# Joined loop of a gated attention: the head variance spread by one block product, and its inverse root made on ScalarE

## The chip, the cores and the metric

The kernel runs on one core of a Trainium2 chip, as one launch. A core has five engines that each work through their own queue in order: TensorE (PE, matrix products into the eight banks of PSUM), VectorE (DVE), ScalarE (ACT), GpSimd (POOL) and SyncE (SP, which issues transfers here). They wait for each other at semaphores alone. The metric is the device time of one execution in microseconds (us); lower is better.

## The reference

Six blocks follow each other on 16 x 64 rows of 512 features. The change lies in the second, a gated linear attention of 16 heads; the third, a linear layer on quantised rows, is computed in the same loop. Cut to what matters:

```
# o: output of the scan, per head of 32 features, plus a sigmoid term
mu = o.mean(-1, keepdims=True)
var = o.var(-1, keepdims=True)
o = (o - mu) * lax.rsqrt(var + EPS)                 # EPS = 1e-5, over the 32 features of a head
o = o.transpose(0, 2, 1, 3).reshape(B, L, -1)
out = jax.nn.silu(g) * o @ Wout
x = x + out
# then, row by row
x = x + (mx_quantize(layernorm(x)) @ mx_quantize(weight).T + bias)   # blocks of 32, 6-bit grid
```

## The kernel before

The 1024 rows are cut into 8 groups of 128. The joined loop of `l0_gated_attention` takes them in a software pipeline: in pass t TensorE attends with group t-1 (`attend_pe`), makes the scores of group t (`scores_pe`), centres group t-1 (`mean_of_pe`), multiplies group t-3 with the output weights (`project_pe`), makes the variance of group t-1 (`variance_pe`), and from pass 5 on runs the linear layer for groups t-5 (`turn_blocks_pe`) and t-6 (`linear_pe`). The attended rows lie turned: the partitions are features, 32 for a head, and the free axis holds four tiles (C = 4) of 128 rows, 512 columns in all. Each engine's order is written out by hand in `tensor`, `vector`, `scalar` and `gpsimd`; `x.wait_ge(signal.s, signal(n))` waits until n+1 events of a signal have come.

How a group g gets its normalisation before the change:

1. `mean_of_pe` takes the head mean away (two products) into bank 5. ScalarE (`square_a`) copies the centred rows into `y` and squares them into `sq`; GpSimd (`gated_pool`) multiplies `y` with the gate.
2. `variance_pe`: four products with `sq` as the stationary side and four columns of `block` (1/32 in each 32 x 32 block of the diagonal) as the moving side. The result has rows on the partitions and 16 heads in 16 columns.
3. `variance_v` (VectorE, L1408) adds EPS into `var`, 128x16. `deviation_pool` (GpSimd, L1093) raises it to -0.5.
4. `widen_a` (ScalarE, L1666) repeats each of the 16 columns 32 times into `wide`, 128x512. `widen_pe` (TensorE, L1155) turns that with four transposes into bank 6.
5. `normal_v` (VectorE, L1413) multiplies `y` with bank 6. `project_pe` (L1163) multiplies the result with the output weights, in fp32, one product for each of the four tiles, into bank 7. `add_v` (L1417) adds that to the rows X, and `stats_of_v` starts the layer norm that feeds the quantisation.

Around this, VectorE masks the scores (`masked_v`), takes the low half of the attended rows (`low_of_v`, through the helper at L320), makes the last gate columns (`gate_last_v`, signal `sg_v`), splits the key weights of the next stage (`key_weights_v`, L320 with tile Wkv), quantises (`quantise_v`) and takes row statistics. ScalarE makes sigmoids of the value term (`sigmoid_a`, L1649), one group a pass, and the high half of the key weights (`key_weights_a`, helper L311). In pass 3 `widen_pe(0)` and `project_pe(0)` wait for the last gate columns. After pass 8 VectorE and TensorE run out the groups still in the pipeline (called the tail below), and the key products and row transposes of the next stage follow.

Other lines that rows name: L1127 and L1130 `attend_pe`, L1114 `scores_pe`, L1139 `mean_of_pe`, L1145 `variance_pe`, L1644 `gate_out_a`, L243 `normalise`, L281 the scaling in the quantisation, L227 row statistics, L1088 `gated_pool`, L1105 `bias_pool`. The tile names W and XT stand for several things: `y`, for one, is a part of W.

Of the kernel before, what the change touches and what calls it, by code (L numbers as in the profile page):

```python
# [13 lines left out]
P = 128  # L14
# [54 lines left out]
def build(nc, a, out):  # L69
# [12 lines left out]
    with ctx:  # L82
# [824 lines left out]
        def l0_gated_attention():  # L907
# [29 lines left out]
            var = sb(ph, "var", [P, 2, GH])  # L937
            half = sb(ph, "mhalf", [P, GH])
# [40 lines left out]
            wide_at = lambda g: y[:, 2, :] if g < 1 else wide[:]  # L979
# [24 lines left out]
            var_v = signal("b_var_v")  # L1004
            rst = signal("b_rst")
            wide_a = signal("b_wide_a")
            wide_pe = signal("b_wide_pe")
# [19 lines left out]
            def gpsimd():  # L1027
                for g in range(G):
                    row_stats_pool(1, g)
                p(pool.memset(half[:], -0.5))  # L1030
# [27 lines left out]
                for t in range(1, G + 1):  # L1058
# [5 lines left out]
                    deviation_pool(t - 1)  # L1064
# [25 lines left out]

            def deviation_pool(g):
                pool.wait_ge(var_v.s, var_v(g))
                pool.tensor_tensor(var[:, g % 2, :], var[:, g % 2, :], half[:], ALU.pow).then_inc(rst.s, 1)  # L1093
# [40 lines left out]
            def mean_of_pe(g):  # L1134
                pe.wait_ge(low_o.s, low_o(g))
                if g:
                    pe.wait_ge(var_v.s, var_v(g - 1))
# [20 lines left out]
            def project_pe(g):  # L1158
                pe.wait_ge(ynm.s, ynm(g))
                if g:  # L1160
                    pe.wait_ge(xsum.s, summed(2, g - 3) if g in (3, 4) else summed(1, g - 1))
                for c in range(C):
                    ins = pe.matmul(bank[:, 7, :], y[:, g % 3, c * P:(c + 1) * P], slot(7)[:, c, :], start=(c == 0), stop=(c == C - 1))  # L1163
                ins.then_inc(proj.s, 1)

            def turn_blocks_pe(g):

                pe.wait_ge(scaled.s, scaled(g))
                if g + 2 < G:
                    pe.wait_ge(ynm.s, ynm(g + 2))  # L1170
# [111 lines left out]
            def tensor():  # L1282
# [121 lines left out]
            def variance_v(g):  # L1404
                dve.wait_ge(var_pe.s, var_pe(g))
                if g >= 2:
                    dve.wait_ge(wide_a.s, wide_a(g - 2))
                dve.tensor_scalar(var[:, g % 2, :], bank[:, 5, 0:GH], EPS, None, ALU.add).then_inc(var_v.s, 1)  # L1408

            def normal_v(g):  # L1410
                dve.wait_ge(wide_pe.s, wide_pe(g))
# [1843 lines left out]
```

## Time and profile before

| | |
|---|---|
| runs | 1156.43, 1158.45, 1624.27 us; median 1158.45 |
| the profiled execution | 1155.84 us, its span 1154.6 us |
| TensorE clock granted | 0.999 of full speed |
| busy in the span | PE 1132.4 us (98%), DVE 749.6 (65%), ACT 537.2 (47%), POOL 244.3 (21%) |
| chain that ended last | PE 88%, DVE 6%, SP's queue 3% |
| the joined loop | first scores at 231.4 us, last key products ahead of the next stage's rows end near 346 us |

The profile is one execution. Busy time of an engine is the time in which an instruction of it ran; the chain is followed back from the last instruction, at each step to what released it. Times of rows are microseconds from the start of the span. TensorE's rows overlap, since products are pipelined: the start of one to the start of the next is what one costs, not its length. An fp32 product is two records and an fp32 transpose one.

### The profile page before, as it was taken

What the parts mean: (1) busy time and instruction counts of PE and PEld (TensorE: products, weight loads), DVE (VectorE), ACT (ScalarE), POOL (GpSimd) and SP (SyncE); (2) the same over time, 40 slices, a digit from 0 to 9 for tenths busy, and PEclk for the clock granted to TensorE, in tenths of its full rate; (3) what the DMA queues carried; (4) which work ended last, traced back from release to release, by engine and by line L of the source; (5) the groups of instructions that cost most, each with busy time, mean ns of one, the idle gap of its engine ahead of it and who ended that gap; (6) DMA issues with size and microseconds to landing.
All of it is one profiled execution on the core that took longest, in us unless ns stands there. A gap on an engine that the chain in (4) does not pass through costs nothing.

```text
span 1154.6 us, 21737 instructions
## 1 busy us (share of the span) xinstructions
PE 1132.4 (98%) x8721; PEld 845.5 (73%) x8721; DVE 749.6 (65%) x1524; ACT 537.2 (47%) x1037; POOL 244.3 (21%) x308
## 2 busy tenths in 40 slices
PE   7999999999999999999999999999999999999997
PEld 4665488776658777777777777777888778887886
DVE  6367478769894656666566666666797876546632
ACT  3244457653222655656565656565554532223421
POOL 2300013266740432121212122221432100000000
PEclk9999999999999999999999999999999999999999
DMA  9759710110205264444444444454810502224211
GB/s 351 273 212 404 278 55 1 40 44 1 110 19 183 40 137 100 92 92 93 92 93 93 92 92 99 91 101 79 112 19 1 83 5 33 37 37 76 34 37 37
DMA packets 325671, 111.57 MB, mean 97 GB/s; under 512 B 301834, under 2 KB 302908, under 8 KB 321348
## 3 DMA queue, kind: packets, MB, share of 16 engines
q1 hardware_dynamic: 324224, 109.11, 37.4%
q8 instruction: 69, 1.13, 0.4%
q10 hardware_dynamic: 1348, 1.09, 0.4%
q14 instruction: 30, 0.25, 0.1%
HBM read 65.59 MB, written 20.97 MB: 75 GB/s over the span
## 4 chain that ended last, share of the span: by engine, by line
PE 88%; DVE 6%; SPq 3%; DMA 1%; issue 1%; ACT 1%; POOL 0%; DVEq 0%; ACTq 0%
PE bank L303 64%; SPq L1871 3%; PE bank L1972 3%; PE bank L583 2%; PE bank L601 2%; PE bank L1988 2%; PE bank L1163 2%; PE bank L259 2%; PE bank L519 1%; PE bank L1185 1%; PE bank L1130 1%; PE bank L1127 1%; PE bank L1114 1%; PE bank L2445 1%; DVE xT L320 1%
## 5 line engine op out<-in xcount | busy, mean ns | idle before, releaser
L1909 POOL COPY PT<-W 32x512 f32<-32x512 f32 x120 | 83.8, 698 | 308.3 <-DVE W L2122 243.4
L2111 DVE CUSTOM_DVE_ANT_0 W<-bank,W 128x512 f32<-128x512 f32 x128 | 80.8, 687 | 101.8 <-PE bank L1972 98.2
L2202 ACT ACTIVATE K<-bank,vecT 128x512 f32<-128x512 f32 x64 | 43.8, 689 | 164.1 <-PE bank L303 164.1
L2223 ACT ACTIVATE W<-W,low 128x512 f32<-128x512 f32 x128 | 90.7, 711 | 16.9 <-DVE low L2111 16.9
L303 PE MATMUL bank<-xT,wT 128*128 128x512 f32 x384 | 92.6, 390 | 0.4 <-DVE wT L320 0.3
L303 PE MATMUL bank<-Wkv,Wq 128*128 128x512 f32 x384 | 92.7, 395 | 0.0
L303 PE MATMUL bank<-Wkv,ctxT 128*128 128x512 f32 x384 | 92.0, 394 | 0.0
L303 PE MATMUL bank<-ctxT,Wkv 128*128 128x512 f32 x384 | 90.1, 392 | 1.2 <-DVE ctxT L320 1.2
L303 PE MATMUL bank<-Wq,Wkv 128*128 128x512 f32 x384 | 89.8, 390 | 0.0
L303 PE MATMUL bank<-woT,hR 128*128 128x512 f32 x384 | 87.8, 390 | 0.6 <-DVE W_late L3081 0.5
L303 PEld LDWEIGHTS bank<-Wkv,ctxT 128*128 128x128 f32 x384 | 70.8, 188 | 22.2 <-ACT K L2202 5.7
L303 PEld LDWEIGHTS bank<-Wkv,Wq 128*128 128x128 f32 x384 | 70.6, 188 | 22.1 <-ACT K L2202 6.5
L303 PEld LDWEIGHTS bank<-ctxT,Wkv 128*128 128x128 f32 x384 | 71.4, 188 | 17.5 <-issue 3.0
L2229 ACT ACTIVATE W<-W,total 128x512 f32<-128x512 f32 x128 | 82.0, 712 | 4.8 <-DVE total L2117 4.8
L303 PEld LDWEIGHTS bank<-woT,hR 128*128 128x128 f32 x384 | 71.9, 188 | 16.4 <-DVE W_late L3081 0.9
L303 PEld LDWEIGHTS bank<-xT,wT 128*128 128x128 f32 x384 | 71.8, 188 | 16.6 <-issue 1.1
L303 PEld LDWEIGHTS bank<-Wq,Wkv 128*128 128x128 f32 x384 | 71.8, 188 | 15.6 <-issue 0.8
L235 POOL TENSOR_TENSOR rstd<-rstd,half_pow 128x1 f32<-128x1 f32 x48 | 30.4, 634 | 212.8 <-DVE rstd L231 212.8
L2122 DVE STREAM_TRANSPOSE W<-W 128x512 f32<-128x512 f32 x120 | 74.5, 675 | 0.2 <-ACT W L2229 0.2
L3185 ACT ACTIVATE h<-bank,vecT 128x512 f32<-128x512 f32 x32 | 22.1, 689 | 89.2 <-PE bank L303 59.9
L303 PE MATMUL bank<-z,BT 128*128 128x512 f32 x192 | 49.1, 391 | 0.6 <-ACT h L3185 0.4
L303 PEld LDWEIGHTS bank<-z,BT 128*128 128x128 f32 x192 | 35.8, 188 | 9.1 <-ACT h L3185 1.8
(378 smaller groups left out, 2117.6 us busy)
## 6 DMA issues: line engine op xcount, KB each, us to landing
PT<-W SPq DMA_DIRECT2D x360, 64.0 KB, 2.1
W<-ctx_turned SPq DMA_DIRECT2D x16, 1024.0 KB, 5.9
W<-in_ctx_dram SPq DMA_DIRECT2D x8, 1024.0 KB, 10.6
ctx_turned<-ctxT SPq DMA_DIRECT2D x8, 1024.0 KB, 7.6
ctx_turned<-W SPq DMA_DIRECT2D x8, 1024.0 KB, 6.7
XT<-in_ctx_dram SPq DMA_DIRECT2D x4, 1024.0 KB, 11.6
XT<-in_L_ffn_wi_dram SPq DMA_DIRECT2D x64, 64.0 KB, 2.1
raw_own<-in_ctx_dram SPq DMA_DIRECT2D x3, 1024.0 KB, 11.0
```

Of the source, the lines that this page charges most:

```text
L235: ins = pool.tensor_tensor(rstd[:, g:g + 1], rstd[:, g:g + 1], half_pow[:], ALU.pow)
L259: ins = pe.transpose(bank[:, first + r, to:to + 32], src_of(t, k)[strip, :], ident[strip, strip])
L303: ins = pe.matmul(dst, stationary(x, k), moving(y, k), start=(first and n == 0), stop=(last and n == len(passes) - 1), skip_group_check=True)
L583: ins = pe.matmul(bank[b * NP:(b + 1) * NP, 4, :], q2T[:, c, j * P + b * NP:j * P + (b + 1) * NP], ctxT[j % 2][:, b, c, :], start=(c == 0) ...
L1871: sp.dma_start(there, here).then_inc(pt_in[half].s, 16)
L1909: pool.tensor_copy(there, here).then_inc(kept_p.s, 1)
L1972: ins = pe.matmul(bank[s2 * NP:(s2 + 1) * NP, 4 + r, :], qT[strip, 2 * rnd + s2, i * NP:(i + 1) * NP], K[strip, 2 * rnd + s2, :], start=Tr ...
L2111: dve.tensor_tensor_reduce(out=PR[:, j, :], in0=bank[:, 4 + j % 4, :], in1=mask, scale=1.0, scalar=3.0e38, op0=ALU.add, op1=ALU.min, accum ...
L2122: dve.transpose(PR[:, j, :], PR[:, j, :]).then_inc(probs.s, 1)
L2202: act.activation(K[:, m, :], bank[:, n % 4, :], ACT.Identity, bias=pcol("L1_xattn_bk", m)).then_inc(ring_a.s, 1)
L2223: act.activation(PR[:, j, :], PR[:, j, :], ACT.Exp, bias=low[:, j:j + 1], scale=-1.0, accum_out=total[:, j:j + 1]).then_inc(expd.s, 1)
L2229: act.mul(PR[:, t, :], PR[:, t, :], total[:, t:t + 1]).then_inc(scaled_p.s, 1)
```

## The change

- `variance_pe` is one product: `block` as the stationary side, `sq` as the moving side, 128x512 in fp32. It gives the variance of each head already repeated on the 32 features, turned as `y` is.
- ScalarE makes the inverse root, with EPS as the bias, into `wide` (now called root). For groups 0 and 1 it copies the variance first (`variance_a`, L1639 of the changed kernel) and takes the root in `early_root_a` (L1646); for the others it takes it straight from bank 5 (L1642), after `normal_v` of the group before has read the buffer.
- `widen_pe`, `widen_a`, `variance_v` and `deviation_pool` are gone.
- `normal_v` reads the root from SBUF. It is made a pass earlier: in pass t for group t-2, and for group 0 at the end of pass 2.
- `project_pe` of groups 0 to 2 is split: its first chunk stands ahead of the mean.
- The sigmoids are all made by pass 2, and the key weights of the next stage a pass later (chunk 0 at the end of pass 2).

```diff
             def variance_pe(g):
                 pe.wait_ge(sqr.s, sqr(g))
-                for t in range(C):
-                    ins = pe.matmul(bank[:, 5, 4 * t:4 * t + 4], sq_at(g)[:, t * P:(t + 1) * P], block[:, 0:P:GDV], start=True, stop=True)
-                ins.then_inc(var_pe.s, 1)
-
-            def widen_pe(g):
-                pe.wait_ge(wide_a.s, wide_a(g))
-                if g:
-                    pe.wait_ge(ynm.s, ynm(g - 1))
-                if g >= 3:
-                    pe.wait_ge(xt_a.s, xt_a(G + g - 3))
-                for t in range(C):
-                    ins = pe.transpose(bank[:, 6, t * P:(t + 1) * P], wide_at(g)[:, t * P:(t + 1) * P], ident[:])
-                ins.then_inc(wide_pe.s, 1)
+                pe.matmul(bank[:, 5, :], block[:], sq_at(g), start=True, stop=True).then_inc(var_pe.s, 1)
...
                 for t in range(G + 3):
                     if t == 1:
                         gate_pe(5)
-                    if t == 3:
-                        pe.wait_ge(sg_v.s, sg_v(1))
-                        widen_pe(0)
                     if 1 <= t <= G:
                         attend_pe(t - 1)
-                    if 4 <= t < G + 3:
-                        widen_pe(t - 3)
...
+                    if t == 3:
+                        pe.wait_ge(sg_v.s, sg_v(2))
+                    if 3 <= t < 6:
+                        project_pe(t - 3, range(1))
                     if 1 <= t < 6:
                         mean_of_pe(t - 1)
...
-                    if t == 3:
-                        pe.wait_ge(sg_v.s, sg_v(2))
                     if 3 <= t:
-                        project_pe(t - 3)
+                        project_pe(t - 3, range(1, C) if t < 6 else range(C))
...
             def normal_v(g):
-                dve.wait_ge(wide_pe.s, wide_pe(g))
+                if g < 2:
+                    dve.wait_ge(root_a.s, root_a(g))
+                else:
+                    dve.wait_ge(var_a.s, var_a(g))
                 dve.wait_ge(gated.s, gated(g))
-                dve.tensor_tensor(y[:, g % 3, :], y[:, g % 3, :], bank[:, 6, :], ALU.mult).then_inc(ynm.s, 1)
+                dve.tensor_tensor(y[:, g % 3, :], y[:, g % 3, :], root_at(g), ALU.mult).then_inc(ynm.s, 1)
...
+            def variance_a(g):
+                act.wait_ge(var_pe.s, var_pe(g))
+                if g < 2:
+                    act.copy(root_at(g), bank[:, 5, :]).then_inc(var_a.s, 1)
+                else:
+                    act.wait_ge(ynm.s, ynm(g - 1))
+                    act.activation(root_at(g), bank[:, 5, :], ACT.Abs_reciprocal_sqrt, bias=eps[:]).then_inc(var_a.s, 1)
+
+            def early_root_a(g):
+                act.wait_ge(var_a.s, var_a(g))
+                act.activation(root_at(g), root_at(g), ACT.Abs_reciprocal_sqrt, bias=eps[:]).then_inc(root_a.s, 1)
...
-                    if t + 1 < G:
-                        sigmoid_a(t + 1)
-                    if 2 <= t < G + 2:
-                        widen_a(t - 2)
+                    if t == 1:
+                        sigmoid_a(2)
+                    elif t == 2:
+                        sigmoid_a(6)
+                        sigmoid_a(7)
                     if t <= G:
                         square_a(t - 1)
                     if t <= 2:
                         gate_out_a(5 + t)
+                    if t == 1:
+                        for g in (3, 4, 5):
+                            sigmoid_a(g)
+                    elif t == 2:
+                        early_root_a(0)
                     if t >= 5:
                         blocks_a(t - 5)
-                    if t <= C:
-                        key_weights_a(t - 1)
+                    if 3 <= t <= 5:
+                        key_weights_a(t - 2)
+                    if t <= G:
+                        variance_a(t - 1)
+                    if t == 2:
+                        early_root_a(1)
+                        key_weights_a(0)
```

The order on TensorE from the variance of group 1 (end of pass 2) to that of group 2 (end of pass 3), before; L1155 is the widening, L1163 the projection:

```order
L1145 MATMUL bank<-block,W 128x4 [waits b_sqr]
L1145 MATMUL bank<-block,W 128x4 x3
L1155 MATMUL bank<-ident,W 128x128 [waits b_wide_a,b_sg_v]
L1155 MATMUL bank<-ident,W 128x128 x3
L1127 MATMUL bank<-Am,V 32x128 [waits c_o_v,b_sig,b_asb]
L1127 MATMUL bank<-Am,V 32x128 x15
L1130 MATMUL bank<-ident,XT 128x128 x4
L1114 MATMUL bank<-W 128x256 [waits b_asb]
L1114 MATMUL bank<-W 128x256 x7
L1139 MATMUL bank<-oT,centring 128x512 [waits b_var_v,c_o_v]
L1139 MATMUL bank<-oT,centring 128x512
L1163 MATMUL bank<-W_early,W 128x512 [waits b_y,b_sg_v]
```

The same place in the changed kernel; L1136 is the variance, L1144 the projection and L1131 the mean:

```order
L1136 MATMUL bank<-W,block 128x512 [waits b_sqr]
L1119 MATMUL bank<-Am,V 32x128 [waits c_o_v,b_sig,b_asb]
L1119 MATMUL bank<-Am,V 32x128 x15
L1122 MATMUL bank<-ident,XT 128x128 x4
L1106 MATMUL bank<-W 128x256 [waits b_asb]
L1106 MATMUL bank<-W 128x256 x7
L1144 MATMUL bank<-W_early,W 128x512 [waits b_y,b_sg_v]
L1131 MATMUL bank<-oT,centring 128x512 [waits b_var_a,c_o_v]
L1131 MATMUL bank<-oT,centring 128x512
L1144 MATMUL bank<-W_early,W 128x512 x3
L1136 MATMUL bank<-sq,block 128x512 [waits b_sqr]
```

The widening ahead of the attention is gone, and a chunk of the projection, which waits for `b_y` (the signal of `normal_v`), has moved ahead of the mean. The order on ScalarE from the gate of pass 2 to the attended rows of group 2 (oT), before:

```order
L1644 ACTIVATE sgT<-bank,vecT 128x512 [waits proj]
L311 CAST Wkv<-W 128x512 [waits slot_in_5]
L311 CAST Wkv<-W 128x512 [waits slot_in_6]
L1653 CAST oT<-bank 128x512 [waits b_ot_pe]
L1649 ACTIVATE XT<-XT 128x512 [waits b_wv]
```

And in the changed kernel, where L1618 is the gate:

```order
L1618 ACTIVATE sgT<-bank,vecT 128x512 [waits proj]
L1646 ACT_TABLE_LOAD
L1646 ACTIVATE W<-W,eps 128x512 [waits b_var_a]
L1639 COPY wide<-bank 128x512 [waits b_var_pe]
L1646 ACTIVATE wide<-wide,eps 128x512 [waits b_var_a]
L311 CAST Wkv<-W 128x512 [waits slot_in_5]
L311 CAST Wkv<-W 128x512 [waits slot_in_6]
L1627 CAST oT<-bank 128x512 [waits b_ot_pe]
```

A table load, two roots and a copy now stand between the gate and the casts of the key weights. It is the one table load that the changed kernel has more. The order on VectorE at the end of the loop, from the last row of the quantisation of group 4 (L285) to the first statistics of the tail, before:

```order
L285 TENSOR_SCALAR W<-XT 128x512 [waits d_scaled,dve_seq]
L1408 TENSOR_SCALAR var<-bank 128x16 [waits b_wide_a,b_var_pe]
L1417 TENSOR_TENSOR X<-X,bank 128x512 [waits proj]
L1413 TENSOR_TENSOR W<-W,bank 128x512 [waits b_gated,b_wide_pe]
L227 BN_STATS stats<-X 128x6 [waits xsum]
```

And in the changed kernel, with L1392 for `add_v` and L1388 for `normal_v`:

```order
L285 TENSOR_SCALAR W<-XT 128x512 [waits d_scaled,dve_seq]
L1392 TENSOR_TENSOR X<-X,bank 128x512 [waits proj]
L1388 TENSOR_TENSOR W<-W,wide 128x512 [waits b_gated,b_var_a]
L227 BN_STATS stats<-X 128x6 [waits xsum]
```

The row that waited for the variance is gone; `normal_v` is that of group 7 instead of 6, and waits for the root of the same group.

## Rows read from the trace of the kernel before

**Rows 1.** Windows: stretch, its length, busy us of each engine, clock, DMA.
```profile
core 0: us, PE busy (x) PEld busy (x) DVE busy (x) ACT busy (x) POOL busy (x), PEclk, DMA share, GB/s
254.00:313.00 59.00, 58.88 (x433) 36.81 (x433) 52.56 (x102) 18.46 (x34) 37.19 (x28) 1.00 0.15 55
313.00:340.00 27.00, 26.56 (x81) 12.70 (x81) 25.19 (x53) 7.11 (x13) 14.25 (x13) 1.00 0.07 20
```

**Rows 2.** Timeline of TensorE, pass 3: start, us, line, operation [idle before <-releaser].
```profile
249.17 0.95 PE L1145 MATMUL bank<-block,W 128*128 128x4 f32 x8
249.98 0.64 PE L1155 MATMUL bank<-ident,W 128*128 128x128 f32 x4
250.55 1.08 PE L1127 MATMUL bank<-Am,V 128*32 128x128 f32 x32
...
254.12 0.74 PE L1139 MATMUL bank<-oT,centring 128*128 128x512 f32 x2 [0.32 <-DVE oT L320]
254.80 3.67 PE L1163 MATMUL bank<-W_early,W 128*128 128x512 f32 x8
258.31 0.95 PE L1145 MATMUL bank<-block,sq 128*128 128x4 f32 x8
259.19 1.08 PE L1127 MATMUL bank<-Am,V 128*32 128x128 f32 x32
```

**Rows 3.** Timeline of ScalarE: a table load, and the gate of pass 2.
```profile
231.39 0.69 ACT L1644 ACTIVATE sgT<-bank,vecT 128x512 f32<-128x512 f32 x1 [2.52 <-PE bank L303]
232.10 1.28 ACT L1649 ACT_TABLE_LOAD   x1
233.39 0.63 ACT L1649 ACTIVATE XT<-XT 128x512 f32<-128x512 f32 x1
...
249.37 0.69 ACT L1644 ACTIVATE sgT<-bank,vecT 128x512 f32<-128x512 f32 x1 [0.98 <-PE bank L303]
249.96 1.13 ACT L311 CAST Wkv<-W 128x512 fp32r<-128x512 f32 x2
```

**Rows 4.** Timeline of VectorE, passes 2 and 3.
```profile
249.37 1.29 DVE L320 TENSOR_TENSOR Wkv<-W,Wkv 128x512 fp32r<-128x512 f32 x2 [0.80 <-PE bank L303]
250.58 0.74 DVE L1401 SCALAR_TENSOR_TENSOR sgT<-bank,vecT,sgT 128x512 f32<-128x512 f32 x1
...
253.98 0.68 DVE L1413 TENSOR_TENSOR W<-W,bank 128x512 f32<-128x512 f32 x1
```

**Rows 5.** Chain of waits, pass 4: start, us, what.
```profile
261.36 0.44 PE bank L1155 x4
```

**Rows 6.** Timelines of TensorE, VectorE and GpSimd, end of pass 8 and tail.
```profile
312.18 0.95 PE L1145 MATMUL bank<-block,sq 128*128 128x4 f32 x8
...
309.44 1.54 DVE L281 TENSOR_TENSOR XT<-XT,inv 128x512 f32<-128x512 f32 x1
...
313.17 0.17 DVE L1408 TENSOR_SCALAR var<-bank 128x16 f32<-128x16 f32 x1 [1.72 <-PE bank L1145]
313.26 0.68 DVE L1417 TENSOR_TENSOR X<-X,bank 128x512 f32<-128x512 f32 x1
...
314.45 0.69 DVE L227 BATCH_NORM_STATS2 stats<-X 128x6 f32<-128x512 f32 x1
...
317.20 1.16 DVE L243 TENSOR_SCALAR W<-X,mv,rstd 128x512 f32<-128x512 f32 x1
...
324.63 0.55 DVE L243 TENSOR_SCALAR XT<-X,mv,rstd 128x512 f32<-128x512 f32 x1 [0.59 <-POOL rstd L235]
...
309.17 1.27 POOL L1088 TENSOR_TENSOR W<-W,sgT 128x512 f32<-128x512 f32 x1 [0.94 <-ACT W L1659]
...
313.42 2.91 POOL L1093 TENSOR_TENSOR var<-var,mhalf 128x16 f32<-128x16 f32 x1 [0.85 <-DVE var L1408]
...
316.81 1.27 POOL L1105 TENSOR_TENSOR X<-X,W 128x512 f32<-128x512 f32 x1
```

More of the change, by code:

```diff
@@ L936, in l0_gated_attention @@
             w = sb(ph, "w2", [P, G, GH])
-            var = sb(ph, "var", [P, 2, GH])
-            half = sb(ph, "mhalf", [P, GH])
+            eps = sb(ph, "eps", [P, 1])
             def xb(h, c, lo, n):
@@ L978, in l0_gated_attention @@
             sq_at = lambda g: W[:, 0, 3, :] if g < 2 else sq[:]
-            wide_at = lambda g: y[:, 2, :] if g < 1 else wide[:]
+            root_at = lambda g: y[:, 2, :] if g < 1 else wide[:]
             by_group = lambda ap: ap.rearrange("f (c g r) -> f (c g) r", c=2, g=G)
@@ L1003, in l0_gated_attention @@
             var_pe = signal("b_var_pe")
[L1004 to L1007, printed above, removed]
+            var_a = signal("b_var_a")
+            root_a = signal("b_root_a")
             gated = signal("b_gated")
@@ L1029, in gpsimd @@
                     row_stats_pool(1, g)
-                p(pool.memset(half[:], -0.5))
+                p(pool.memset(eps[:], EPS))
                 p(pool.memset(augw[:], 0.0))
@@ L1089, in gated_pool @@
                                    ALU.mult).then_inc(gated.s, 1)
-            def deviation_pool(g):
-                pool.wait_ge(var_v.s, var_v(g))
-                pool.tensor_tensor(var[:, g % 2, :], var[:, g % 2, :], half[:], ALU.pow).then_inc(rst.s, 1)
             def scale_pool(g):
@@ L1136, in mean_of_pe @@
                 if g:
-                    pe.wait_ge(var_v.s, var_v(g - 1))
+                    pe.wait_ge(var_a.s, var_a(g - 1))
                 for h in range(2):
@@ L1143, in variance_pe, with project_pe @@
                 pe.wait_ge(sqr.s, sqr(g))
-                for t in range(C):
-                    ins = pe.matmul(bank[:, 5, 4 * t:4 * t + 4], sq_at(g)[:, t * P:(t + 1) * P], block[:, 0:P:GDV], start=True, stop=True)
-                ins.then_inc(var_pe.s, 1)
-            def widen_pe(g):
-                pe.wait_ge(wide_a.s, wide_a(g))
-                if g:
-                    pe.wait_ge(ynm.s, ynm(g - 1))
-                if g >= 3:
-                    pe.wait_ge(xt_a.s, xt_a(G + g - 3))
-                for t in range(C):
-                    ins = pe.transpose(bank[:, 6, t * P:(t + 1) * P], wide_at(g)[:, t * P:(t + 1) * P], ident[:])
-                ins.then_inc(wide_pe.s, 1)
[L1158 to L1164, printed above, removed]
+                pe.matmul(bank[:, 5, :], block[:], sq_at(g), start=True, stop=True).then_inc(var_pe.s, 1)
+            def project_pe(g, chunks=range(C)):
+                if 0 in chunks:
+                    pe.wait_ge(ynm.s, ynm(g))
+                    if g:
+                        pe.wait_ge(xsum.s, summed(2, g - 3) if g in (3, 4) else summed(1, g - 1))
+                for c in chunks:
+                    ins = pe.matmul(bank[:, 7, :], y[:, g % 3, c * P:(c + 1) * P], slot(7)[:, c, :], start=(c == 0),
+                                    stop=(c == C - 1), skip_group_check=True)
+                if C - 1 in chunks:
+                    ins.then_inc(proj.s, 1)
             def turn_blocks_pe(g):
                 pe.wait_ge(scaled.s, scaled(g))
-                if g + 2 < G:
-                    pe.wait_ge(ynm.s, ynm(g + 2))
                 if g:
@@ L1532, in vector @@
                         low_of_v(t - 1)
-                    if 3 <= t:
-                        normal_v(t - 3)
                     for r in range(4):
                         masked_v(t, r)
+                    if 3 <= t:
+                        normal_v(t - 2)
                     if t in (6, 7):
@@ L1545, in vector @@
                         gate_last_v(5 + t)
+                    if t == 2:
+                        normal_v(0)
                     if t in (3, 6, 7):
                         key_weights_v({3: 1, 6: 2, 7: 3}[t])
-                    if 1 <= t:
-                        variance_v(t - 1)
                     if 3 <= t:
@@ L1557, in vector @@
                 low_of_v(7)
-                normal_v(5)
+                normal_v(6)
                 quantise_v(4)
-                variance_v(7)
                 for g in (5, 6, 7):
                     add_v(g)
-                    if g < 7:
-                        normal_v(g + 1)
+                    if g == 5:
+                        normal_v(7)
                     stats_of_v(1, g)
@@ L1660, in square_a @@
                 act.activation(sq_at(g), bank[:, 5, :], ACT.Square).then_inc(sqr.s, 1)
-            def widen_a(g):
-                act.wait_ge(rst.s, rst(g))
-                if g:
-                    act.wait_ge(wide_pe.s, wide_pe(g - 1))
-                act.copy(wide_at(g).rearrange("p (h d) -> p h d", h=GH),
-                         var[:, g % 2, :].unsqueeze(2).broadcast_to([P, GH, GDV])).then_inc(wide_a.s, 1)
+            def variance_a(g):
[8 more added lines that the diff above has]
+                act.activation(root_at(g), root_at(g), ACT.Abs_reciprocal_sqrt, bias=eps[:]).then_inc(root_a.s, 1)
             def blocks_a(g):
@@ L1764, in scalar @@
                         gate_out_a(5 + t)
+                    if t == 1:
[3 more added lines that the diff above has]
+                        early_root_a(0)
                     if t >= 5:
                         blocks_a(t - 5)
-                    if t <= C:
-                        key_weights_a(t - 1)
+                    if 3 <= t <= 5:
+                        key_weights_a(t - 2)
+                    if t <= G:
+                        variance_a(t - 1)
+                    if t == 2:
+                        early_root_a(1)
+                        key_weights_a(0)
                     if t == G + 3:
```

6 lines of the change are left out of this document (removed).

## The prediction

> **What bounds the kernel now.** I read the page first: TensorE is busy 98% of the span and the chain that ended last is TensorE for 88%. The change touches one stretch of some 110 us of the 1154.6, so I asked for busy times by stretch. From 254 to 313 us, the middle of the joined loop, TensorE is busy 58.88 of 59 us and VectorE 52.56: TensorE sets the pace and VectorE is close behind. From 313 to 340 us both are nearly full, 26.56 and 25.19 of 27 [rows 1]. Who leads there is told by the chain of waits and the timeline of VectorE: VectorE waited 1.72 us for the narrow products of the last group, and from there the chain runs through VectorE and GpSimd [rows 6]. So two things count: TensorE's own time up to the last variance product, and how soon after it VectorE gets going.
>
> **TensorE's work.** A widening is four 128x128 transposes and is worth 0.44 us in the chain [rows 5]; its start-to-start time in the third pass is 0.57 us (249.98 to 250.55) [rows 2]. All eight go. Six of them (groups 0 to 5) stand ahead of the last variance product, two behind it. The four narrow variance products (128x4 out of 128x128 weights) take 0.88 us from start to start (258.31 to 259.19). The one product of 512 columns that replaces them is of the same kind as those of L1163, of which four take 3.51 us (254.80 to 258.31), so 0.88 us each [rows 2]. I cost this exchange at nothing; if the switch from one kind to the other costs or saves 0.1 us, eight make plus or minus 0.8 us.
>
> **The new wait in pass 3.** Before, TensorE waited 0.32 us here, for the low half of the attended rows (254.12) [rows 2]. Now the first chunk of the projection of group 0 stands ahead of the mean, and it waits for VectorE's `normal_v(0)`. That is queued behind `key_weights_v(0)` and `gate_last_v(7)`, and the key weights are now queued on ScalarE behind both early roots. Step by step:
> - ScalarE starts the gate of u=7 at 249.37 and takes 0.69 us. A table load followed such a gate 0.71 us after its start (231.39 to 232.10), and the next instruction started 1.29 us after the load (233.39) [rows 3]. So the load stands at 250.08 and the first root at 251.37.
> - A root reads a 128x512 tile with a bias from memory, as the gate does: 0.69 us, with the next start 0.6 us on (249.37 to 249.96) [rows 3]. No row shows this function; the bounds are the 0.63 us of the sigmoid, and 0.69. The copy of the variance of group 1 starts at 251.97 and ends at 252.60, since I give it the sigmoid's 0.63; the second root needs it and ends at 253.29.
> - The two casts of the key weights take 1.13 us together [rows 3], the first ending about 253.8, the second about 254.3.
> - VectorE's second split then ends about 255.0 (two take 1.29 us), the gate's product (0.74 us) about 255.65, and `normal_v(0)` (0.68 us) about 256.3 [rows 4].
>
> TensorE would be ready early: variance product of group 1 at 249.17, 0.88 us, then the 3.25 us that lie between 250.55 and 253.80 (254.12 less the wait), so 253.30 [rows 2]. It stalls 3.05 us, against 0.32 before. Then one chunk (0.88), the mean (0.68), three chunks (2.63): the variance product of group 2 starts at 256.35 + 4.19 = 260.5 instead of 258.31, so 2.2 us late [rows 2]. The low half of group 2 is late too, but VectorE makes it right after `normal_v(0)`, within the 0.88 us of the chunk.
>
> **Passes 4 to 8.** Five widenings go, 5 x 0.44 = 2.2 us. The normalisation of a group is now made a whole pass ahead of its projection, so no new stall. VectorE's work per pass is the same but for 0.17 us of the row that added epsilon (L1408, hidden today by other waits) [rows 6]. At the last variance product (312.18 before) the sum is 2.2 - 2.2 = 0, within 0.1.
>
> **The tail.** VectorE no longer waits for the variance before adding group 5, but `normal_v(7)`, the next row, does: product 312.18 + 0.88, some 0.15 to its end (the four narrow ones: start 312.18, used at 313.17), the root 0.69, so 313.9; the normalisation 0.6; statistics at 314.5, where they stand now (314.45) [rows 6]. So 0 again. What is left is GpSimd: without the power of 2.91 us at 313.42, the bias of group 4 (now 316.81) comes up to 0.8 us sooner, when the statistics it is queued behind are ready. Today it lies on the normalisation at 317.20, which takes 1.16 us where the one at 324.63 takes 0.55 [rows 6]. That frees between 0 and 0.6 us; I take 0.4, being nearer to the freed case. `normal_v(7)` also leaves its old place, 0.6 us later in the tail, but VectorE then waits for GpSimd (0.59 us at 324.63 [rows 6]), whose chain starts from the same quantisation, so I count nothing for it. Behind the loop there is no edit: the later stages start sooner by what the loop ends sooner, as TensorE has no idle time of size there.
>
> **The sum**: + 2.2 (pass 3) - 2.2 (widenings) + 0 (products) - 0.4 (collision gone) = -0.4 us, on the profiled execution's own 1155.84 (span 1154.6 and 1.2 around it): 1155.4. The three runs shown have the median 1158.45; the one of 1624.27 left out, the other two and the profiled one lie at 1155.84, 1156.43 and 1158.45, middle 1156.4. A median of undisturbed runs of the changed kernel should then be 1156.0.
>
> **What the skill says against it.** The table load took 1.28 us and the next instruction followed 0.01 us later; ahead of it stood 0.02 us [rows 3]. The Trainium skill (ScalarE: Activation LUTs, What ACT_TABLE_LOAD costs) gives 1283 ns for the load, which the row bears out, and 1380 ns of drain on top, which the row does not show. By its sum the stall of pass 3 would be 1.4 us longer and the total +1.0 us, an estimate.
>
> **Rivals.**
> - The stall is hidden (chance 0.15). If ScalarE's roots and casts came early enough, only the savings remain: 6 x 0.44 ahead of the last product plus the 0.32 us wait and 0.4, so -3.4 us: 1153.0 on the same footing. Against it: the chain has nine links in series and the first cannot start before 249.37.
> - Slower by a collision of memory reads (chance 0.13). `normal_v` read one operand from PSUM and took 0.68 us; now both lie in SBUF. The product of L281, which has both in SBUF, took 1.54 us at 309.44 beside GpSimd's gate at 309.17 [rows 6]. If `normal_v` met GpSimd's work at each of the last six groups, VectorE would need 6 x 0.86 = 5.2 us more, less the slack that it has in passes 4 to 8, 59 - 52.56 = 6.4 in all but mostly spent on waits in the first of them [rows 1]; about half would reach the end: +2.2 us, 1158.6. It decides from three hits in passes 6 to 8. Against it: GpSimd has been relieved of 2.91 us a pass. In a sentence of its own: the Trainium skill (GPSIMD Engine Reference, Specifications) names just this sharing for VectorE instructions with two SBUF inputs; the row at 309.44 agrees.
> - The load costs as a drained switch does (chance 0.1). If the first root starts 1.4 us later than the row of 232.10 says, each link behind it does too: +1.0 us, 1157.4.
> - The change has no further effect than to trade waits, and the collision of 317.20 stays (chance 0.12): 0 to +0.3 us, 1156.5.
>
> That leaves 0.5 for the forecast.
>
> **How the numbers follow.** The bounds of the unknown costs are 0.8 us either way for the products and 0.4 for the roots; the likeliest case spans 1154.5 to 1157.5. With the hidden stall below and the collision above, and the 2.6 us over which the undisturbed runs of before spread, the range is 1152.5 to 1160. Within 2% means 23 us, about what a measurement of this kernel can tell from no change; no case reaches a sixth of it. The loop would have to lose or gain a fifth of its length, which only a mechanism that I don't see could do: same 0.98, faster 0.01, slower 0.01.
>
> **What would show it.** In the profile after: no L1155-like transposes in the loop beyond the turned blocks; one more table load on ScalarE near 250.1 with no gap behind it; TensorE idle about 3 us near 253.3, ended by VectorE's normalisation; the variance product of group 2 near 260.5, and that of group 7 near 312.2; the second statistics of the tail near 314.5; a wait on the root ahead of the normalisation of group 7; the normalisation near 317 at about 0.55 us. The forecast is wrong if that stall is under 2 us or over 4, if the wide product takes other than 0.8 to 1.0 us, or if `normal_v` takes over 1 us in passes 6 to 8.

## The result and the profile after

The changed kernel takes 1160.76 us (median of 7 runs, 1159.22 to 1161.61) against 1156.86 for the kernel before (median of 7, of which one took 1624.27), a ratio of 1.0034 with the interval 1.0023 to 1.0045. It is slower by 3.9 us, within 2%, where I forecast 0.4 us less and a range that ended at 1160. The profiled execution has a span of 1159.5 us against 1154.6.

The time that TensorE waited, summed by what it waited for, the three longest waits of the changed kernel:

```profile
engine line waited for: us in total, times, longest us
PE bank L513 <- DMA W<-in_L_xattn_kernel_k_dram: 9.4, 1, 9.4
PE bank L1144 <- DVE W L1388: 3.3, 1, 3.3
PE bank L1978 <- issue: 2.3, 3, 0.9
```

The same view of the kernel before:

```profile
PE bank L513 <- DMA W<-in_L_xattn_kernel_k_dram: 7.7, 1, 7.7
...
PE bank L1988 <- issue: 1.1, 2, 0.8
```

The first row, the load at the very start, is chance: in the run `after_again` below the same kernel had its first product at 7.75 us, like the kernel before at 7.68. The rows of the loop stand 2.6 us late in the profiled execution after: 1.7 us from this load, and 0.9 us that came between the first product and the first attend product (228.54 us apart, 227.63 before and 227.68 in `after_again`). So I compare from the first attend product on (237.94 us; 235.32 before). The second row is the stall that I forecast. The third I had not thought of: TensorE stands in the attention of a later stage (L1978, L1988 before) and waits for nothing that the profile shows.

The stall in pass 3, timeline of TensorE after (start, us, line, operation [idle before <-releaser]):

```profile
254.91 1.15 PE L1106 MATMUL bank<-W 32*128 32x256 f32 x16
259.31 1.10 PE L1144 MATMUL bank<-W_early,W 128*128 128x512 f32 x2 [3.26 <-DVE W L1388]
259.85 1.02 PE L1131 MATMUL bank<-oT,centring 128*128 128x512 f32 x2
260.70 2.73 PE L1144 MATMUL bank<-W_early,W 128*128 128x512 f32 x6
263.28 1.02 PE L1136 MATMUL bank<-sq,block 128*128 128x512 f32 x2
```

Timelines of ScalarE and VectorE after, the chain that makes it:

```profile
252.76 1.28 ACT L1646 ACT_TABLE_LOAD   x1
254.06 0.72 ACT L1646 ACTIVATE W<-W,eps 128x512 f32<-128x512 f32 x1
254.69 0.57 ACT L1639 COPY wide<-bank 128x512 f32<-128x512 f32 x1
255.28 0.72 ACT L1646 ACTIVATE wide<-wide,eps 128x512 f32<-128x512 f32 x1
255.91 1.12 ACT L311 CAST Wkv<-W 128x512 fp32r<-128x512 f32 x2
...
256.61 1.29 DVE L320 TENSOR_TENSOR Wkv<-W,Wkv 128x512 fp32r<-128x512 f32 x2 [5.35 <-ACT Wkv L311]
257.82 0.74 DVE L1379 SCALAR_TENSOR_TENSOR sgT<-bank,vecT,sgT 128x512 f32<-128x512 f32 x1
258.49 0.68 DVE L1388 TENSOR_TENSOR W<-W 128x512 f32<-128x512 f32 x1
```

VectorE is idle for 5.35 us behind a table load, a copy, two roots and a cast, and TensorE for 3.26 us behind VectorE. Against [rows 2] the variance product of group 2 starts 2.35 us later (counted from the first attend product, as all shifts here). It is 1.91 us late in pass 4, 1.83 in pass 5, then 1.46, 1.10 and 0.73 at group 7. The tail, timeline of VectorE after, for the last rows of [rows 6]:

```profile
317.31 0.69 DVE L1388 TENSOR_TENSOR W<-W,wide 128x512 f32<-128x512 f32 x1 [0.89 <-ACT wide L1642]
317.92 0.69 DVE L227 BATCH_NORM_STATS2 stats<-X 128x6 f32<-128x512 f32 x1
...
320.68 0.54 DVE L243 TENSOR_SCALAR W<-X,mv,rstd 128x512 f32<-128x512 f32 x1
```

Here the statistics are 0.86 us late, the normalisation takes 0.54 us where it took 1.16, and the next stage's first query product is 0.23 us late. So in this execution the loop costs 0.23 us. But the kernel is 3.9 us slower: most of the loss is elsewhere.

### The profile page after: what moved, and what is told of

The parts are those of the page before. It is cut to its first block, busy times and chain, and to the rows that moved or that the text cites. A ratio compares the mean times of both kernels' runs of the same rounds, so it can differ in the third digit from the quotient of the medians.

```text
span 1159.5 us, 21548 instructions
## 1 busy us (share of the span) xinstructions
PE 1130.4 (97%) x8641; PEld 838.1 (72%) x8641; DVE 749.1 (65%) x1516; ACT 539.9 (47%) x1040; POOL 222.9 (19%) x300
## 3 DMA queue, kind: packets, MB, share of 16 engines
q8 instruction: 69, 1.13, 0.4%
## 4 chain that ended last, share of the span: by engine, by line
PE 89%; DVE 6%; SPq 2%; ACT 1%; DMA 1%; issue 1%; POOL 0%; DVEq 0%; ACTq 0%
PE bank L303 65%; PE bank L1962 3%; PE bank L583 2%; PE bank L601 2%; PE bank L1978 2%; PE bank L259 2%; SPq L1861 2%; PE bank L1144 1%; PE bank L519 1%; PE bank L1166 1%; DMA W<-in_L_xattn_kernel_k_dram 1%; DVE stats L227 1%; PE bank L249 1%; PE bank L2435 1%; PE bank L1122 1%
```

## The experiments

The ratios are to the kernel before, measured in the same session and on the same chip (1156.65 to 1156.69 us in the three sessions). "Loop" is the time from the first attend product to the first query product of the next stage; "behind the loop" is from there to the start of TensorE's last product.

### Both kernels again

No edit.

> The kernel before, unchanged, profiled once more: how much of the 4.9 us between the two profiled executions is one execution against another. Theory O (the opening is chance): the first weight load (6.3 us to landing before, 8.0 after) and with it TensorE's first row (7.7 us before, 9.4 after) vary from execution to execution, here anywhere from 7.5 to 9.5. Rival (the opening goes with the program): again within 0.3 us of 7.7. Theory F (instruction fetch): TensorE's idle times in the attention of the next stage, behind no wait, come back at the same places as before (435.5, 522.1, 549.3 us, 1.6 us in all), since the instruction stream is the same. Ratio 1.000 +- 0.001.

> The changed kernel, unchanged, profiled once more. Theory O: TensorE's first row anywhere from 7.5 to 9.5 us. Rival: again near 9.4. Theory F: TensorE's idle times behind no wait come back at the same places (418.2, 746.9, 774.2, 803.9 us, 2.8 us in all), apart from a common shift. Ratio to before about 1.003.

Before again: 1156.66 us. After again: 1160.14 us, 1.0031 (1.0019 to 1.0043). Loop 120.46 us before (120.44 in the first profile), 122.34 after, where the first profile of the same kernel had 120.67. Timeline of TensorE, `after_again`:

```profile
256.81 1.21 PE L1144 MATMUL bank<-W_early,W 128*128 128x512 f32 x2 [3.26 <-DVE W L1388]
257.34 1.53 PE L1131 MATMUL bank<-oT,centring 128*128 128x512 f32 x2
258.67 3.94 PE L1144 MATMUL bank<-W_early,W 128*128 128x512 f32 x6
```

The stall is 3.26 us as before, but the same six product records take 3.94 us and not 2.73. Windows over these products (stretch, its length, busy us by engine, PEclk, DMA), of `after_again`:

```profile
256.80:262.40 5.60, 5.59 (x10) 2.71 (x11) 5.32 (x8) 2.11 (x4) 1.81 (x1) 0.70 0.01 3
...
258.00:260.00 2.00, 2.00 (x5) 1.15 (x4) 2.00 (x4) 1.09 (x3) 0.43 (x1) 0.50 0.00 0
```

and of the first profile of the changed kernel:

```profile
259.30:263.30 4.00, 3.99 (x11) 2.00 (x12) 4.00 (x6) 2.11 (x4) 1.28 (x1) 1.00 0.00 0
```

The granted clock fell to half (0.50 is the level of 1.2 GHz) behind the stall in one execution and not in the other, and it costs 1.67 us (122.34 - 120.67). The Trainium skill (TensorE: Matmul & The Clock Gate, Part 1) says of the slow products at a kernel's start that their number differs from run to run of the same kernel; these two profiles show the like behind a stall in the middle of one.

The first product came at 7.68 and 7.75 us in these two. In the other runs it came between 7.45 and 7.83 us, but at 9.45 in `after_filled`: the late opening is chance and goes with neither kernel.

### The position of TensorE's instruction stream

The two rows of "issue" above stand at different times in the two kernels. The page lists a DMA queue that brings instructions, the same row in both kernels:

```profile
q8 instruction: 69, 1.13, 0.4%
```

69 pieces in 1.13 MB are 16 KB each. The trace of the changed kernel has 17606 instructions of TensorE, which makes 64 bytes an instruction and 256 instructions a piece. The change takes 169 instructions out of TensorE's stream (80 products with their weight loads, and 9 waits), so every piece boundary behind the loop moves. In `after_pad169` they are given back as waits that are met long before, spread over the wide products of the loop (two calls of `wait_ge` become one instruction, hence the factor 2 in the code; the trace has 492 waits for 323); `before_pad87` puts 87 into the kernel before, which is the same position as taking 169 away, as a piece holds 256 (256 - 169 = 87).

```diff
+            padded = {"left": 169, "sites": 64}
+            def pad_pe():
+                n = -(-padded["left"] // padded["sites"]) if padded["sites"] else 0
+                padded["left"] -= n
+                padded["sites"] -= 1
+                for _ in range(2 * n):
+                    pe.wait_ge(ready_v.s, ready_v(2))
...
+                    pad_pe()
                     ins = pe.matmul(bank[:, 7, :], y[:, g % 3, c * P:(c + 1) * P], slot(7)[:, c, :], start=(c == 0),
```

> The changed kernel with 169 waits that are long met, spread ahead of the 64 wide products of the joined loop, so that TensorE's stream has as many instructions ahead of the next stage as before the change (it has 169 fewer: 80 weight loads, 80 products, 9 waits). Nothing computed is changed. Theory F: the idle times of 0.7 to 0.9 us at 746.9, 774.2 and 803.9 go and those of the kernel before come in their place (near 435, 522 and 549): 1.0 to 2 us faster than the changed kernel, ratio to before 1.0015 to 1.0025. Rival (the waits or transfers of the next stage are late for another reason than the fetch): same idle times as after, ratio 1.0034 or more, as the waits cost up to 0.05 us each where nothing hides them.

> The kernel before with 87 such waits in the joined loop. A fetch brings 256 instructions, and 169 fewer stand at the same place in a fetch as 87 more. Theory F: the next stage then shows the idle times of the changed kernel (three of 0.7 to 0.9 us near 745, 771 and 800) and loses those near 435, 522 and 549: 1 to 2 us slower than before, ratio 1.001 to 1.002. Rival: idle times as before, ratio 1.000.

After with 169: 1158.30 us, 1.0015 (1.0006 to 1.0025), so 1.8 us less than the changed kernel. Before with 87: 1159.20 us, 1.0025 (1.0016 to 1.0034), so 2.5 us more than the kernel before (forecast 1 to 2), with no useful work changed; its loop keeps 120.32 us. Timeline of TensorE in the changed kernel, the attend product of the later stage near 745 us:

```profile
744.07 1.99 PE L1978 MATMUL bank<-PT,V 128*32 128x64 f32 x126
746.92 0.27 PE L1978 MATMUL bank<-PT,V 128*32 128x64 f32 x2 [0.87 <-issue]
```

The same place in `after_pad169`:

```profile
745.27 1.99 PE L1990 MATMUL bank<-PT,V 128*32 128x64 f32 x128
747.19 0.50 PE L303 MATMUL bank<-Wkv,Wq 128*128 128x512 f32 x1
```

And `before_pad87`, which has the kernel before's code but stands at the changed kernel's places, and at one more near 438 us:

```profile
438.40 0.54 PE L2000 MATMUL bank<-PT,W 128*32 128x64 f32 x22 [1.16 <-issue]
...
745.26 0.27 PE L2000 MATMUL bank<-PT,V 128*32 128x64 f32 x2 [0.90 <-issue]
...
772.51 0.31 PE L2000 MATMUL bank<-PT,W 128*32 128x64 f32 x5 [0.73 <-issue]
```

In such a block 128 products of 64 columns and their weight loads, 256 instructions, run in 2 us. The idle time comes 2 products ahead of the block's end or 5, to the same number in `before_pad87` and in the changed kernel.

That TensorE waits there for the next piece of its program is borne out by a count over all fourteen profiles of this document. They have 38 idle times of over 0.25 us without a wait behind the loop. Count TensorE's instructions (products, weight loads, waits) that were recorded ahead of each: 8642 and 9154 in the kernel before, 12737, 13249 and 13762 in the changed one, 10177, 10690 and 11202 in `keys_spread_p113` below. Divided by 256, all 38 counts leave 193 or 194. And all 38 idle times end 2.2 to 2.9 us after the transfer of a piece has begun (after: begun at 744.25, end of the idle time at 746.92). What no run shows is why only a few of the 69 pieces come late, and how late: at one place (8642) three executions of one stream stood for 0.34, 0.72 and 0.32 us (before, before again, and `before_late0` below), and at the place of 438 us the changed kernel did not stand, where `late_keys` and `keys_spread` below, with as many instructions ahead, stood for 1.16.

So the number of instructions ahead decides where TensorE can stand, and this is worth up to 2.5 us here. The time behind the loop is 791.8 and 792.4 us (before, before again), 793.2 and 793.5 (after, again), 792.1 (after with 169), 794.2 (before with 87); the idle times over 0.25 us make up most of these differences, not all. (`before_late0`, with the stream of before, has 790.7.)

### The clock behind the stall

`after_filled` lets TensorE work while it would stand, and releases nothing sooner. The three products go to a free bank and are not read.

```diff
                     if t == 3:
+                        pe.wait_ge(sg_v.s, sg_v(1))
+                        for _ in range(3):
+                            pe.matmul(bank[:, 6, :], ident[:], slot(7)[:, 0, :], start=True, stop=True,
+                                      skip_group_check=True)
                         pe.wait_ge(sg_v.s, sg_v(2))
```

> The changed kernel with three wide fp32 products of no use (the identity with a chunk of the out weights, into a bank that is free then), put on TensorE ahead of the wait of the first out product, so that TensorE works through about 2.7 of the 3.26 us in which it stood; nothing is released sooner. Theory (the slow products behind the stall come from the granted clock, which falls after TensorE has stood for 3.26 us): the clock is 1.00 from 255 to 264 us, the six out products take 2.7 us and not 3.94, the loop takes 120.7 us and not 122.3, and the time is 1158.5 us against 1160.2. Rival 1 (they were slow for another reason, such as reads of the same memory by the engines that run then): they stay at 3.9 us, time 1160.2. Rival 2 (the fillers end later than the wait): slower than 1160.2 by what they overrun.

1157.62 us, 1.0010 (1.0001 to 1.0019): 2.5 us less than the changed kernel, for more work. Timeline of TensorE, and in a second fence the window behind the wait:

```profile
255.36 2.84 PE L1306 MATMUL bank<-W_early,ident 128*128 128x512 f32 x6
258.69 1.10 PE L1144 MATMUL bank<-W_early,W 128*128 128x512 f32 x2 [0.49 <-DVE W L1393]
```

```profile
258.70:262.70 4.00, 4.00 (x11) 2.00 (x12) 4.00 (x7) 2.11 (x4) 1.27 (x1) 1.00 0.00 0
```

Full clock, loop 120.66 us. The forecast of 1158.5 was 0.9 high; the filling also moves the stream, by 12 instructions in the trace, and of the three idle times of the later stage the one near 803 us (0.72) is gone.

`before_late0` puts a stall into the kernel before:

```diff
                     if 3 <= t:
+                        if t == 3:
+                            for _ in range(5):
+                                v(dve.tensor_tensor(xq[:, 0, :], X[:, 0, :], X[:, 0, :], ALU.add))
                         normal_v(t - 3)
```

> The kernel before with five additions of no use (X+X into free rows, 128x512, 0.69 us each) on VectorE ahead of the first normalisation (normal_v(0) in pass 3), so that the ready normalised group, and TensorE's first out product, come about 3.4 us late; nothing else is changed, and the instruction stream of TensorE is the one before. Theory (the stall by itself costs its own length and, in most executions, the clock behind it): TensorE idle 3.2 to 3.6 us ahead of the first out product, granted clock near 0.5 for 3 to 5 us behind it, loop 120.4 + 3.4 + 1.7 = 125.5 us, time 1161.8 us. Rival (a stall of this length is made up by TensorE's slack in passes 4 to 8, or the clock fell for another reason that only the changed kernel has): clock 1.00 throughout, loop 120.4 to 123.8 us, time 1157 to 1160.

1163.57 us where 1161.8 was forecast, 1.0062 (1.0049 to 1.0075), loop 127.09. The five additions took 4.53 us, not 3.4. Timeline of TensorE, and in a second fence the window over the products:

```profile
259.15 5.70 PE L1163 MATMUL bank<-W_early,W 128*128 128x512 f32 x8 [4.53 <-DVE W L1413]
```

```profile
259.10:264.70 5.60, 5.55 (x9) 2.41 (x10) 3.50 (x6) 0.00 (x0) 0.00 (x0) 0.63 0.01 3
```

The eight records took 3.67 us in [rows 2] and take 5.70 here. Loop: 120.44 + 4.53 + 2.03 = 127.00. Nothing of the stall was made up in passes 4 to 8, and nothing of the changed kernel is needed for the clock to fall.

### The stall itself

`late_keys` takes the cause of the stall out of pass 2.

```diff
                     if t == 2:
                         dve.wait_ge(proj.s, proj(GATE + 7))
-                        key_weights_v(0)
...
-                    if t in (3, 6, 7):
-                        key_weights_v({3: 1, 6: 2, 7: 3}[t])
+                    if t in (3, 4, 6, 7):
+                        key_weights_v({3: 0, 4: 1, 6: 2, 7: 3}[t])
...
-                    if 3 <= t <= 5:
-                        key_weights_a(t - 2)
+                    if 3 <= t <= 6:
+                        key_weights_a(t - 3)
...
                         early_root_a(0)
-                        key_weights_a(0)
```

> The changed kernel with the four chunks of key weights rounded and split one pass later (chunk 0 in pass 3 and not in pass 2), so that in pass 2 ScalarE goes from the two early roots straight to the attended copy and VectorE does not wait for the rounded key weights ahead of its gate and its first normalisation; all else as in the changed kernel. Theory (the stall and what hangs on it is one of two causes): TensorE's idle time ahead of the first out product falls from 3.26 us to under 0.8, no stretch behind it is granted less than the full clock, and the loop (first attend product to the first query product) takes near 119 us in place of 122.3 (120.7 in the execution without the clock loss); the time is 1155.5 us (1160.2 - 3.0 - 1.7), and the products of the later stages where TensorE stands without a wait (746, 773, 803 us) still do so, 3 us earlier. Rival (VectorE bounds the loop in passes 4 to 8, busy 9.7 us in ten): the stall goes, but the loop's end comes no more than 1 us earlier, and the time is 1158.5 or more.

> The kernel of the run late_keys with 169 long-met waits spread ahead of 64 wide products of TensorE's loop, as in after_pad169, which bring the instruction stream behind the loop back to the positions it has in the kernel before. Theory (the two causes, the stall in the loop and the position of the stream, are separate and add up): 1.8 us below late_keys (after_pad169 against after_again: 1158.3 against 1160.1), 1153.7 us, faster than both kernels; idle without a wait at 521 and 549 us, none at 743 to 801. Rival (the two share a cause, or the waits cost time of their own in a loop that has no stall): the same as late_keys or slower.

1158.19 us (1.0012, 1.0004 to 1.0021) and 1156.52 us (1.0000, 0.9991 to 1.0009). Both forecasts failed, by 2.7 and 2.8 us (1155.5 and 1153.7). The stall in pass 3 is gone, but the loop takes 119.85 us, not 119.0, and with 169 waits 121.48; behind the loop `late_keys` takes 794.2 us, with the 1.16 us near 438.7 told of above. Timelines of TensorE and VectorE in `late_keys`, two passes later (VectorE's split stands at the end of pass 4):

```profile
272.17 1.10 PE L1144 MATMUL bank<-W_early,W 128*128 128x512 f32 x2 [1.58 <-DVE X L1392]
273.84 0.73 PE L1131 MATMUL bank<-oT,centring 128*128 128x512 f32 x2 [0.57 <-DVE oT L320]
...
269.29 2.14 DVE L320 TENSOR_TENSOR Wkv<-W,Wkv 128x512 fp32r<-128x512 f32 x2
271.35 0.68 DVE L1392 TENSOR_TENSOR X<-X,bank 128x512 f32<-128x512 f32 x1
```

I had put a split into pass 4, where VectorE has none in either kernel: it took 2.14 us (1.29 in pass 2; GpSimd was at work all through it, from 269.45 to 272.55), `add_v(1)` behind it was late, and the next out product needs its bank. A wait was traded for another. In the run with 169 waits the clock fell behind these waits (there 1.53 and 0.61 us) too:

```profile
272.00:279.00 7.00, 6.39 (x15) 3.04 (x14) 6.79 (x14) 2.60 (x5) 1.95 (x3) 0.76 0.01 2
```

`keys_spread` moves the splits on, with the cast order of `late_keys`; the other two differ from it in the position of the stream alone.

```diff
-                    if t in (3, 4, 6, 7):
-                        key_weights_v({3: 0, 4: 1, 6: 2, 7: 3}[t])
+                    if t in (3, 6, 7):
+                        key_weights_v({3: 0, 6: 1, 7: 2}[t])
...
                 normal_v(6)
                 quantise_v(4)
+                key_weights_v(3)
```

> As late_keys, but VectorE splits the key weights' chunks 0 to 3 in passes 3, 6, 7 and behind pass 8 (between the last normalisation of a group's rows there and add_v(5)), not in passes 3, 4, 6 and 7. Theory (late_keys lost its gain to VectorE: the split put into pass 4 took 2.14 us, so that add_v(1) was late, and with it TensorE's out product of group 2 by 1.58 us and the mean of group 4 by 0.57): both idle times go, the loop takes near 117.8 us in place of 119.85, and the time is 1156.0 us against late_keys' 1158.2. Rival (VectorE bounds these passes as a whole, and the wait comes back in a later pass or in the tail): loop 119.5 or more and time 1158.

> keys_spread with 169 long-met waits in TensorE's loop, so that the instruction stream behind the loop stands where it does in the kernel before. Theory: 1.8 to 2 us below keys_spread by the position of the stream, near 1154.1 us, which is 0.998 of the kernel before. Rival (the waits cost time where TensorE does not stand): the same as keys_spread.

> keys_spread with 113 such waits in place of 169: only the position of the stream differs. Theory (TensorE's idle times without a wait follow from where the pieces of 256 instructions fall in the dense attend products): the loop is that of keys_spread_p169 within 0.1 us, the idle times without a wait are at other places or of other lengths than with 0 and with 169 waits, and any difference of the times is their sum. No size is forecast from outside: the three positions measured so far differ by 0 to 2.5 us, so 1153.5 to 1157. Rival (the waits' number costs, not the position): between keys_spread and keys_spread_p169.

1156.05 us (0.9993, 0.9984 to 1.0002), 1153.29 us (0.9975, 0.9965 to 0.9985) and 1156.10 us (0.9998, 0.9989 to 1.0006). The loops are 117.79, 117.78 and 117.73 us, so all the rest lies behind them: 794.2, 792.0 and 794.7 us. The forecasts were 1156.0, 1154.1 and 1153.5 to 1157. It is the position and not the number of the waits that counts, for 113 of them gave nothing and 169 gave 2.8 us. With 113 waits the three idle times lie in stretches where none lay before. Timeline of TensorE, `keys_spread_p113`:

```profile
602.57 0.31 PE L1989 MATMUL bank<-PT,W 128*32 128x64 f32 x6 [1.28 <-issue]
...
632.78 0.53 PE L1989 MATMUL bank<-PT,V 128*32 128x64 f32 x21 [1.16 <-issue]
...
660.28 0.54 PE L1989 MATMUL bank<-PT,W 128*32 128x64 f32 x24 [1.09 <-issue]
```

and `keys_spread_p169`, at the places of the kernel before:

```profile
519.65 0.42 PE L1989 MATMUL bank<-PT,V 128*32 128x64 f32 x12 [0.70 <-issue]
...
546.89 0.43 PE L1989 MATMUL bank<-PT,W 128*32 128x64 f32 x15 [0.79 <-issue]
```

`keys_spread_p169` is 3.4 us faster than the kernel before and 7 us faster than the changed one.

### The sum closed

`after_filled` with 156 waits: the stall stays, the clock is held, the stream stands as before.

> The changed kernel with the three useless products in the stall (as after_filled) and 156 long-met waits, which with the 13 instructions that the filling adds bring the stream's position behind the loop to that of the kernel before; the stall itself stays. Theory (the whole loss of the change is the clock behind the stall and the position of the stream; the stall's length and the saved widenings cancel, as forecast): within 1 us of the kernel before, 1156.7 to 1157.2 us, loop 120.7, clock 1.00 from 250 to 270 us, idle without a wait near 523 and 551 us only. Rival (something else in the changed kernel costs as well): 1158 or more.

1156.83 us, 0.9999 (0.9990 to 1.0008), loop 120.55. Idle without a wait at the places of the kernel before alone. (The filling and the waits make 168 instructions in the trace, one short of 169.) With the clock and the stream put right the changed kernel is the kernel before, to 0.2 us. By medians the stream is worth 1.8 us (1160.14 to 1158.30) and the clock, at this position of the stream, 1.5 (1158.30 to 1156.83).

## Why the prediction was wrong, step by step

- **Behind the loop: this step failed.** "The later stages start sooner by what the loop ends sooner" is not so. I read it from the absence of large idle times and looked for edits only. The 169 instructions that the change takes out of TensorE's program shift where it stands in the dense attend blocks: 1.8 us (1160.14 against 1158.30).
- **The stall's price: half of this step failed.** The stall came with the links in the order that I gave: forecast 3.05 us, measured 3.26; group 2's variance product forecast 2.2 us late, measured 2.35. I charged it its length. It also costs TensorE's clock: 1.7 us where it fell (122.34 against 120.67), 1.5 in the medians. With the 1.8 above that is 3.3 to 3.5 us, of the 1160.14 - 1156.65 = 3.5 measured.
- **Passes 4 to 8: right in kind, too large.** Forecast -2.2 us, measured 2.35 - 0.73 = 1.62. Pass 4 gave the 0.44. Pass 5 gave 0.08, for the mean of its pass waited for VectorE's low half: from the first chunk of the projection to the variance product TensorE took 4.83 us (275.54 to 280.37), 0.28 more than for the same products before (271.38 to 275.93). "No new stall" was wrong there. The last three gave 0.36 or 0.37 each.
- **The exchange of products, costed at nothing**, is at most 0.1 us a product: in `late_keys` the wide product starts at 258.28 and the attend product behind it at 259.23, 0.95 us where the four narrow ones took 0.88 [rows 2]. That is the 0.07 that the last three passes lack.
- **Roots and load.** Root forecast 0.63 to 0.69 us, measured 0.72 out of SBUF and 0.69 out of PSUM. Table load 1.28 us and the next instruction 0.02 us behind it, as in [rows 3]. The drain that the Trainium skill (ScalarE: Activation LUTs, What ACT_TABLE_LOAD costs) adds is not in this trace either: that rival is out.
- **The tail: right.** The collision was gone, the normalisation 0.54 us for 1.16, so 0.62 where I took 0.4. The statistics came 0.13 us later than group 7's variance product accounts for (0.86 against 0.73), where I had none.
- **The hidden stall** did not occur; VectorE's 5.35 us of waiting shows how far it was from it. `keys_spread` shows what it would have been worth: its loop is 2.7 us shorter than before (117.79 against 120.46), where the rival said 3.4.
- **The collision of `normal_v`** occurred in passes 3 to 5 (1.32, 1.47 and 1.01 us) and in none of passes 6 to 8 (0.68), the line I had drawn. It cost at most the 0.28 us of pass 5.
- **The range** took in each cost that I had named, at its bounds, and its upper end of 1160 held neither of the two that I had not. Either of them alone would have been inside. None of the four rivals names either of the two.

In the loop of the first profile the sum was -0.4 forecast and +0.23 measured. From my 1156.0 to the 1160.76 of the result it is then 0.5 (the kernel before has 1156.86 by all its runs, where I took 1156.4), 0.6 (this sum) and 3.3 to 3.5 (the two terms that were missing).

## What to carry to other kernels

Charge a stall of TensorE of three microseconds with its length and with the clock of the products behind it, and if it can't be removed, fill it with products of no use. When engine orders are changed, move an instruction only to a pass where its engine has idle time ahead of the next consumer. And where a change adds or removes some instructions of TensorE (169 here), look at the dense blocks behind it for idle time without a releaser, and try a few counts of harmless instructions before a difference of one or two microseconds is put down to the change itself.

## What the runs showed of the hardware

- With the same stall the granted clock stayed at full in one profile (3.26 us) and went to half, 0.50 for some 3 us, in two others (3.26 and 3.22); behind 1.58 and 0.57 us of idle time it stayed in one profile, and behind 1.53 and 0.61 it fell in another. Which it will be in one execution isn't settled by these runs.
- TensorE idles for 0.3 to 1.3 us behind nothing that the profile names, inside blocks that go through 256 instructions in 2 us, at places set by the number of instructions ahead of them: all 38 such times, in fourteen profiles, stand at the same place in a piece of 256 instructions, and end 2.2 to 2.9 us after the transfer of a piece has begun. Three positions of one kernel differed by 2.8 us (1153.29, 1156.05 and 1156.10).
- Spread over TensorE's loop, 87 waits that were long met cost it nothing (120.32 us against 120.46).
- A VectorE instruction with both operands in SBUF took 0.68 us alone and up to 1.47 beside GpSimd (the normalisations of the changed kernel); five additions, partly beside it, took 0.91 each on average.
